# Recommendation tower on one Trainium2 core: the gathers of a turn paced by the matmuls of the held tables

## The reference, cut to what matters

```python
e = jnp.stack([tbl_0[ids[:, 0]], ..., tbl_25[ids[:, 25]]], axis=1)      # 26 lookups per sample, 2048 samples
combined = jnp.concatenate([dense[:, None, :], e], axis=1)              # 27 features of 128
interactions = jnp.einsum('bfd,bgd->bfg', combined, combined)
z = interactions[:, iu, ju]                                             # 351 pairs above the diagonal
h = jnp.concatenate([z, dense], axis=1)                                 # 479
h = jnp.maximum(h @ W_top1 + b_top1, 0.0)                               # 512
h = jnp.maximum(h @ W_top2 + b_top2, 0.0)                               # 256
y = h @ W_top3                                                          # 1
```

## Time and profile before

| | |
|---|---|
| median of 3 runs | 391.25 us (389.94 to 393.21) |
| the profiled execution: time | 389.43 us |
| its span, first to last instruction | 387.6 us |
| mean granted TensorE clock | 0.987 of full speed |
| TensorE busy | 356.0 us of the span (92%) |
| GpSimd busy | 224.1 us (58%) |
| a turn in the loop (turns 2 to 6) | 42.6 to 44.1 us |

### The profile page before, as it was taken

How to read it: one execution, slowest core, us unless ns; L and a number is a source line. 1 busy time by engine, 2 the same in 40 slices (tenths; PEclk the granted TensorE clock), 3 DMA queues, 4 the chain that set the end, 5 groups by cost and what they waited for, 6 DMA issues and landing times.

```text
span 387.6 us, 14627 instructions
## 1 busy us (share of the span) xinstructions
PE 356.0 (92%) x6468; PEld 336.2 (87%) x6468; DVE 283.1 (73%) x197; ACT 158.5 (41%) x270; POOL 224.1 (58%) x228
## 2 busy tenths in 40 slices
PE   0999778998959999999999989999999999999995
PEld 0888768997859998999989988999989988998894
DVE  3999999992749927994869845993969756992440
ACT  2456532343423444434542454344433354334422
POOL 5747653666426764567735765666736763766500
PEclk9999989999969999999999999999999999999999
DMA  6999213412223112321223214221233113211100
GB/s 186 282 278 300 84 33 95 104 42 53 64 71 98 47 47 65 102 84 47 66 93 90 47 47 121 60 82 48 64 100 93 47 52 104 74 47 49 46 20 2
DMA packets 22607, 33.30 MB, mean 86 GB/s; under 512 B 6111, under 2 KB 14943, under 8 KB 22587
## 3 DMA queue, kind: packets, MB, share of 16 engines
q1 hardware_dynamic: 15234, 18.26, 16.3%
q0 software_dynamic: 7168, 14.69, 14.6%
q10 hardware_dynamic: 186, 0.09, 0.1%
HBM read 29.93 MB, written 0.01 MB: 77 GB/s over the span
## 4 chain that ended last, share of the span: by engine, by line
PE 71%; DMA 10%; issue 7%; POOL 5%; SPq 3%; ACT 1%; POOLq 1%; DVE 1%; DVEq 0%
PE psum L553 35%; PE psum L579 11%; PE psum L568 6%; PE psum L669 5%; POOL rows L294 5%; DMA lows<-table 4%; DMA rows<-table,idx 4%; PE psum L592 3%; PE psum L593 3%; PE psum L594 3%; PE psum L541 2%; PE psum L677 2%; SPq L235 2%; POOLq L68 1%; SPq L202 1%
## 5 line engine op out<-in xcount | busy, mean ns | idle before, releaser
L294 POOL DMA_INDIRECT rows<-table,idx x224 | 223.9, 999 | 140.0 <-issue 63.1
L322 DVE TENSOR_TENSOR onehot<-ids_b,psum 125x2048 fp32r<-125x2048 int16 x97 | 216.2, 2279 | 5.9 <-DMA ids_b<-hot_ids 5.5
L412 ACT ACTIVATE feats<-psum 128x512 f32<-128x512 f32 (+2 forms) x120 | 79.6, 710 | 133.2 <-PE psum L553 110.1
L553 PE MATMUL psum<-onehot,hot_hi 125*128 125x256 f32 x736 | 109.4, 292 | 1.7 <-issue 1.2
L553 PE MATMUL psum<-onehot,hot_lo 125*128 125x256 f32 x736 | 103.3, 283 | 0.0
L553 PEld LDWEIGHTS psum<-onehot,hot_hi 125*128 125x128 f32 x736 | 95.5, 191 | 3.6 <-issue 1.9
L302 DVE COPY gram<-psum 26x416 f32<-26x416 f32 x64 | 37.4, 584 | 82.3 <-PE psum L579 80.8
L553 PEld LDWEIGHTS psum<-onehot,hot_lo 125*128 125x128 f32 x736 | 95.3, 192 | 0.0
L579 PEld LDWEIGHTS psum<-feats 128*26 128x26 f32 x4096 | 41.3, 103 | 19.2 <-issue 15.4
L579 PE MATMUL psum<-feats 128*26 128x26 f32 x4096 | 46.6, 193 | 12.1 <-issue 8.6
L412 ACT ACTIVATE gram<-psum 26x416 f32<-26x416 f32 (+1 forms) x72 | 35.6, 494 | 21.4 <-PE psum L579 11.5
(11 more groups left out here) (37 smaller groups left out, 172.3 us busy)
## 6 DMA issues: line engine op xcount, KB each, us to landing
lows<-table SPq DMA_DIRECT2D x12, 448.0 KB
ids_b<-hot_ids SPq DMA_DIRECT2D x8, 512.0 KB
rows<-table,idx POOLq DMA_INDIRECT x224, 2.5
ids_b<-hot_ids SPq DMA_DIRECT2D x8, 256.0 KB, 3.7
rows<-dense SPq DMA_DIRECT2D x16, 64.0 KB, 3.6
lows<-w SPq DMA_DIRECT2D x1, 1024.0 KB, 23.3
lows<-table SPq DMA_DIRECT2D x12, 52.0 KB
pairs<-gram SPq DMA_DIRECT2D x16, 39.0 KB
```

The costliest lines, as they stand in the source:

```text
L294: pool.indirect_dma_start(out=rows[:, f, :], out_offset=None, in_=tables[f - 1], in_offset=bass.IndirectOffsetOnAxis(ap=idx[:, 2 * s + t, ...
L322: nc.vector.tensor_tensor(onehot[f % SLOTS][0:HP_ROWS, :, :], ids_b[0:HP_ROWS, f:f + 1, :].to_broadcast([HP_ROWS, HC, SB]), psum[0:HP_ROWS ...
L412: return nc.scalar.activation(o, x, ACT.Copy)
L553: mm = nc.tensor.matmul(psum[:, bank, m * SB:(m + 1) * SB], part[0:HP_ROWS, f, c, :], onehot[f % SLOTS][0:HP_ROWS, c, :], start=(part is h ...
```

## The change

All edits are in POOL's program. The three pauses for landings are gone. Eight gathers now wait for held features of their own turn: (0,10) for number 4, (0,12) for 5, (0,14) for 6, (1,2) for 7, (1,4) for 8, (1,6) for 9, (1,8) for 10 and (1,10) for 11. The gate on the second gram stands before (0,6) and no longer before (0,4). The gate before (1,12) stays.

```diff
-    PAUSES = [(0, 2), (1, 0), (1, 2)]
+    NOT_BEFORE = {(0, 10): 4, (0, 12): 5, (0, 14): 6, (1, 2): 7, (1, 4): 8, (1, 6): 9, (1, 8): 10, (1, 10): 11}
...
-            def wait_landed(s, t, g):
-
-                if g > 0:
-                    wait_gathered(pool, s, t, g - 1)
-                elif t == 1:
-                    wait_gathered(pool, s, 0, NG - 1)
...
                         wait_rows_free(pool, s, t, g)
-                        if s > 0 and (t, g) in PAUSES:
-                            wait_landed(s, t, g)
-                        if s > 0 and t == 0 and g == 1:
-
-                            pool.wait_ge(gram_done[1], 2 * s)
                         if s > 0 and t == 1 and g == NG - 1:
 
                             pool.wait_ge(gram_done[1], 2 * s + 1)
                         for f in features:
+                            if s > 0 and (t, f) in NOT_BEFORE:
+                                pool.wait_ge(hot_done, NH * s + NOT_BEFORE[t, f] + 1)
+                            if s > 0 and (t, f) == (0, 6):
+
+                                pool.wait_ge(gram_done[1], 2 * s)
```

## The result

The changed kernel takes 389.11 us (median of 20 runs, 387.56 to 390.87) against 390.87 us before (20 runs, 389.74 to 393.21). The ratio is 0.9947, 95% interval 0.9928 to 0.9966: 0.5% faster, which on 390.87 us is 2.1 us. The forecast was 1.6 us less.

The account below looks back on a forecast made before the run. TensorE's own instructions bound the kernel, plus late gathers, matmuls slowed by gathers, and accidents. Terms -1.0 (turn 4), -0.5 (first grams), -0.5 (tail), +0.4 (turn 0) sum to -1.6 us, median 391.25 to 389.6 us; range 386.4 to 393.0.

Parts of the forecast that it names:

- What bounds a turn: Whole loop: TensorE's own instructions, plus late gathers, accidents and 0.44 us for each gather that starts inside a gram.
- The gate two gathers later: Gate moved to (0,6): (0,4), (0,5) precede the second gram; 0 in turns 1 to 6, +0.4 us at turn 0's end.
- The wait of (0,10): POOL before (0,10): holds about 3.3 us but leaves the gather where it was; not on the path, 1.7 us left.
- POOL runs a whole gather ahead of the first gram: Faster rival: one or more of three gathers leaves the first gram; -2.6 us more, 387.0 us; two, 384.4; chance 0.13.
- The seven other waits: POOL, (0,11) to (1,14): held features end 0.5 us or more before their gathers need them; cost nothing.
- The pauses: Three landing pauses on POOL: removal gives some 2.2 us a turn, group 2 comes earlier; turn 4 -1.0 us.
- The first gram: First gram of each turn: (1,5) stretched by L331, again three gathers in the gram; -0.5 us in all.
- the inference of the page: Descriptor generation not stalled by two-input tensor_tensor: (1,5) unstretched, first-gram term -1.2 instead of -0.5, 388.9 us; chance 0.03.
- The tail: End of turn 7: last gather issue ends 1.2 us earlier, rows 1,3 no longer wait 0.39 us; -0.5 us.

## Why the prediction was right, and where it was not

The sum was -1.6 us and -2.1 us were measured (-1.3 to -2.8 by the interval). That they come so close is in part luck: turns 0 and 1 alone moved by 2.9 us between the two profiled executions. (The prediction's 388 to 391.3 us by the bounds isn't their sum: added up, without the one for two gathers in each second gram, they give 387.0 to 393.3.) Step by step:

*What bounds a turn*: right. TensorE's own instructions, plus what gathers do to the grams. The price of 0.44 us was too low for a gather that lies wholly inside a gram. The sum divided by three gathers, but the first of them started at 353.08 us, 0.04 us ahead of the gram (353.12), and a first gram with none takes 2.36 us, not 2.40. The runs give 0.55 to 0.58 us for each later one, 0.30 for one right at the start, and nothing for memsets.

*The gate two gathers later*: 0 in turns 1 to 6, shown by second grams of 2.40 us, but closer than reckoned. L332, the old L338, caught (0,3) and stretched it to 1.28 us, and (0,5) was still being issued when the gram began; I had 0.8 us left. At the end of turn 0, +0.4 was forecast for two gathers in the gram. In the profiled execution neither started in it, but 1.37 and 0.12 us ahead. The gram took 5.20 us against 4.63 before and 4.60 with the gate at (0,4), but its own stop took 1.75 us where the others' took 1.39 and 1.61, so the +0.6 can't be put down to gathers. Two other kernels had both gathers at that gram, from -0.10 and from 0.40 us on: 5.07 and 5.37 us, with stops of only 0.89 and 0.93. That is +0.4 to +0.8 us, with part of it hidden in a shorter stop, as the prediction had it. Another kernel's gram of 5.12 us there, with one gather, shows how uneven that turn is.

*The wait of (0,10)*: its mechanism was right (idle 3.78 us, (0,10) where it was), and as a difference to before it does cost nothing. But I took "not on the path" as the end of it, because rows 0,2 had 1.7 us in hand, and did not ask what the gathers 10 to 20 us further back would gain without the wait. They would have left the first gram. The rival "POOL runs a whole gather ahead of the first gram" had the mechanism, and a price of 0.44 us each that was on the low side, and I left it at "1.2 us more than I find" although POOL's idle 3.3 us stood two paragraphs above. Without the wait the kernel takes 383.46 us, 7.8 less than before and 5.7 to 6.1 less than with it (389.1 to 389.5).

*The seven other waits*: cost nothing. Shown by the kernel that keeps only the first.

*The pauses*: the size was right for turn 4 (43.6 to 42.4 us), though its first gram grew from 2.90 to 3.52 us on the way. The cause was right only in part. With the pauses alone taken out turn 4 stays 0.6 us longer than its neighbours, and with the gate back at (0,4) 0.4 us longer; (0,4) starts late there in both. Alone the pauses bring 0.9898, more than the change does, though the intervals overlap.

*The first gram*: the step failed in its detail, not its size. I had (1,5) stretched by L331 in most turns. It started 0.05 us before that operation (179.07 against 179.12 in turn 3), took 0.95 us, and was not stretched. So (1,9) came at T + 24.8 us and not at 25.7, and two gathers start in the gram, not three: it lasts 3.50 us. In turns 2, 3, 5, 6 and 7 the first grams are 0.02 to 0.29 us shorter, 0.8 in all, where I took -0.5. In turn 4 the gram is longer, as said.

*On the inference of the page*: the Trainium skill (SBUF — State Buffer, "Who interferes with whom") infers that a `tensor_tensor` doesn't stall the building of descriptors. Gathers that started inside the one over the pairs took up to 1.72 us in these kernels (0.94 us is usual), 1.28 us beside L332, and 3.54 us beside L369 although that one started 0.44 us after the gather. All of them ended 0.75 to 0.83 us after the operation. The trace disagrees with the inference for a gather. But a gather also reads its row numbers from SBUF (`idx`), and the same section lets `tensor_tensor` contend with reads; no run tells the two apart. The section's rule that PE never waits for another engine agrees with the memsets (2.36 us). Beside gathers the grams take longer (2.66 to 4.59 us). The section speaks of SBUF's ports, and no run shows whether it is a port that holds the weight loads.

*The tail*: -0.5 forecast; T to the last gram went from 40.6 to 39.7 us, of which 0.2 is the first gram, so -0.6.

With the terms as measured: turn 4 -1.2 (its longer gram included), the other first grams -0.8, tail -0.6, together -2.6 us. For turn 0 the forecast's +0.4 stands neither confirmed nor refuted by this execution, and turn 1 (49.50 to 50.11 us) differs by the granted clock as well.

## What to carry to other kernels

A wait that puts an instruction where it stood before still has a price if the same edit has just taken away the reason to stand there: follow the idle time to the end of the queue, and ask what could have left a sensitive stretch. Time the sensitive stretch by itself (here one gram of 256 matmuls with and without a gather), because a gap of 0.2 us inside it is invisible in a busy share of 92%. When waits are added by a rule, test them one by one; here one of eight did anything, and what it did was a loss of about 6 us, 1.5%. It took back what another edit of the same change, the gate's move, had gained.

## What the runs showed of the hardware that was not expected

A gather started on GpSimd slows a run of 26-column matmuls by 0.30 to 0.58 us, in gaps of 0.2 us between weight loads just after its start. Twelve memsets on the same engine during the whole gram cost nothing (2.36 us). Beside 256-column matmuls gathers cost nothing: eight of them take 1.10 us in turn 4 of the changed kernel both with a gather started in them (204.61) and with POOL idle (206.50). The moving of the rows is not it (a gather that lands in the gram costs nothing), nor the last half of the issue. Which part of the first half microsecond does it was not tried.

A gather that starts inside a DVE operation with two SBUF inputs is held to 0.75 to 0.83 us past the end of it, in every case from turn 1 on in which it would have ended sooner. One that starts 0.05 to 0.30 us before the operation over the pairs (0.95 us long) is free, one that started 0.44 us before the longer L369 (2.27 us) was held (3.54 us). This was not explained.

On two occasions the kernel before took 474 to 475 us instead of 391, with TensorE halting for 0.3 to 2 us between matmuls that wait for nothing the profile shows. The mean granted clock of these executions was 0.89 to 0.91, against 0.97 to 1.00 otherwise.
